# Turning the normalised x2 by two transposing DMAs instead of eight PE transposes and an ACT copy

## The reference

```python
x = x + 0.5 * ffn(layernorm(x))    # first expert layer
x = x + attn(layernorm(x))         # differential attention, 16 heads, 4 key/value heads, causal
x = x + 0.5 * ffn(layernorm(x))    # second expert layer, same weights

def ffn(x):                        # xf: 4096 tokens x 512
    logits = xf @ router_w + router_b          # 16 experts
    S = softmax(logits)
    G, idx = top_k(S.T, 256)                   # each expert takes its 256 best tokens
    out = xf[idx] @ expert_w + expert_b        # one weight matrix for all experts
    y = zeros.at[idx].add(G * out)
```

## Time and profile before

| | |
|---|---|
| time, median of 3 runs | 1959.65 us (1959.47 to 1966.55) |
| the profiled execution | 1976.26 us |
| its span, first to last instruction | 1974.5 us |
| granted TensorE clock over the span | 0.835 of full speed |
| instructions | 44298 |

### The profile page before, as it was taken

One profiled execution on the slowest core, in us unless ns is written; L12 is line 12 of the kernel. 1 busy time (PEld: TensorE's weight loads), 2 busy tenths in 40 slices (PEclk: granted clock), 3 DMA queues, 4 the chain that ended last, 5 costly groups with the idle time before them and its releaser, 6 DMA issues. The chain is left out here.

```text
span 1974.5 us, 44298 instructions
## 1 busy us (share of the span) xinstructions
PE 1514.6 (77%) x10639; PEld 1050.2 (53%) x10682; DVE 1446.2 (73%) x5493; ACT 1259.9 (64%) x3422; POOL 1098.9 (56%) x1507
## 2 busy tenths in 40 slices
PE   2897434478888988888988888988988988885520
PEld 2543212256666666666666666666666766663210
DVE  6568211588789899889888898988899767751168
ACT  2253112488778888888878888888788767762120
POOL 4321222366567777768776777777777555552200
PEclk9899666788889898989998998999899667666655
DMA  7013311111111111111111111211111100000077
GB/s 283 1 47 129 108 34 42 34 27 36 32 29 52 47 41 41 50 47 49 44 52 41 47 41 47 52 47 43 47 47 41 38 21 16 16 16 32 32 259 265
DMA packets 179670, 117.25 MB, mean 59 GB/s; under 512 B 139170, under 2 KB 139554, under 8 KB 179619
## 3 DMA queue, kind: packets, MB, share of 16 engines
q1 hardware_dynamic: 179618, 116.65, 20.0%
HBM read 51.57 MB, written 33.55 MB: 43 GB/s over the span
## 5 line engine op out<-in xcount | busy, mean ns | idle before, releaser
L1401 ACT ACTIVATE ex<-bank,nbias 128x512 f32<-128x512 f32 (+3 forms) x1024 | 528.8, 539 | 64.9 <-DVE bank L1120 62.5
L1120 DVE TENSOR_SCALAR_CACHE_REDUCE bank<-bank,nesc 128x512 f32<-128x512 f32 (+3 forms) x1024 | 503.3, 551 | 61.5 <-PE bank L1547 60.9
L1577 PEld LDWEIGHTS bank<-vs,pr 128*128 128x128 f32 x2560 | 339.7, 208 | 22.8 <-issue 12.8
L1577 PE MATMUL bank<-vs,pr 128*128 (+1 forms) x2560 | 344.1, 286 | 8.4 <-issue 4.1
L1559 PE MATMUL bank<-cst,df 128*128 128x128 f32 x1280 | 267.2, 312 | 85.5 <-ACT pr L1418 84.8
L1300 POOL TENSOR_SCALAR ex<-ex,gam 128x128 f32<-128x128 f32 (+3 forms) x512 | 318.8, 635 | 0.0
L1545 PE MATMUL bank<-ks,qs 96*128 (+2 forms) x1024 | 266.4, 337 | 48.9 <-ACT ex L1401 46.7
L1418 ACT ACTIVATE pr<-bank 128x128 f32<-128x128 f32 (+3 forms) x512 | 232.3, 454 | 95.7 <-PE bank L1559 94.7
L1146 DVE CUSTOM_DVE_ANT_0 df<-ex 128x128 f32<-128x128 f32 (+3 forms) x512 | 259.8, 522 | 8.4 <-issue 3.7
L1559 PEld LDWEIGHTS bank<-cst,df 128*128 128x128 f32 x1280 | 170.5, 168 | 112.2 <-ACT pr L1418 95.6
L1401 ACT ACTIVATION_READ_ACCUMULATOR ex<-bank,nbias 128x1 f32 x1024 | 223.5, 218 | 0.0
(11 more groups left out here) (272 smaller groups left out, 2960.2 us busy)
## 6 DMA issues: line engine op xcount, KB each, us to landing
qs<-turned SPq DMA_DIRECT2D x384, 64.0 KB, 2.1
x_dram<-xa SPq DMA_DIRECT2D x8, 1024.0 KB, 4.9
b_xs<-x_dram SPq DMA_DIRECT2D x32, 256.0 KB, 2.7
x<-x_dram SPq DMA_DIRECT2D x32, 256.0 KB, 2.6
x_dram<-x SPq DMA_DIRECT2D x32, 256.0 KB, 2.0
y_dram<-scratch SPq DMA_DIRECT2D x32, 256.0 KB, 2.0
c_x<-x_dram SPq DMA_DIRECT2D x8, 1024.0 KB, 14.5
c_y<-y_dram SPq DMA_DIRECT2D x8, 1024.0 KB, 15.2
```

The source lines that it names most:

```text
L1120: dve.tensor_scalar(part, part, nesc[:, 0:1], None, ALU.mult, ALU.min, accum_out=nbias[:, j, i, a:a + 1]).then_inc(bias_done.sem, 1)
L1401: ac.activation(ex[j % 4][:, a, lo:hi], energy(j, i)[:, a, :], ACT.Exp, bias=nbias[:, j, i, a:a + 1], scale=-1.0, accum_out=esum[:, j, i, ...
L1577: mm = pe.matmul(bank[:, 7, t * DV:(t + 1) * DV], pr[j % 2][:, lo + k * P:lo + (k + 1) * P], val, start=(k == 0), stop=(k == t))
```

## The change

The eight PE transposes of `turn_x2` and the ACT copy `take_x2` go. SP gets a function `turn_x2` between the reload of x2 and the store of y: it waits for `product_o` (which reads the buffer that is overwritten) and for `low2`, and issues two DMAs with `transpose=True`, one for each f16 half, from `split[:, a, HEADS]` to `xt2`, block by block. `route` on PE waits for both DMAs of its tile (32 increments of the new semaphore `xt2_in`). ACT's writes into `split[:, 0, HEADS]` for later tiles (`rope_high(0)`, `high_heads`), which waited for the PE turn of the tile before, wait for its DMAs.

```diff
@@ -989,7 +989,7 @@
                 "rstd2_done"), sig("xn2_done")
             hi2_done, lo2_done, xt2_done, xt2_out = sig("hi2_done"), sig("lo2_done"), sig("xt2_done"), sig("xt2_out")
             route_done, lg_out, y_done, y_out = sig("route_done"), sig("lg_out"), sig("y_done"), sig("y_out2")
-            x2_st, y2_st = sem2("x2_st"), sem2("y2_st")
+            x2_st, y2_st, xt2_in = sem2("x2_st"), sem2("y2_st"), sem2("xt2_in")
             x1_t = x1_d.rearrange("b (t p) e -> (b t) p e", p=P)
             x2_t = x2_d.rearrange("b (t p) e -> (b t) p e", p=P)
             y2_t = y2_d.rearrange("b (t p) e -> (b t) p e", p=P)
@@ -1064,6 +1064,12 @@
                     x2_done.wait(sp, u, apart_s)
                     sp.dma_start(flat(x2_t[ds(u, 1), :, :]), x2[:, :]).then_inc(x2_st, 16)
 
+                def turn_x2(u):
+                    o_done.wait(sp, u, apart_s)
+                    lo2_done.wait(sp, u, apart_s)
+                    for a in range(2):
+                        sp.dma_start(xt2[:, a, :].rearrange("p (k n) -> p k n", k=KT), split[:, a, HEADS].rearrange("p (k n) -> p k n", k=KT), transpose=True).then_inc(xt2_in, 16)
+
                 def store_y(u):
                     y_out.wait(sp, u, apart_s)
                     sp.dma_start(flat(y2_t[ds(u, 1), :, :]), yb[:, :]).then_inc(y2_st, 16)
@@ -1090,6 +1096,7 @@
                     store(K - BEHIND)
                     if again:
                         load_again(K - (BEHIND - 1))
+                    turn_x2(K - BEHIND)
                     store_y(K - BEHIND)
                     if u is not None:
                         stack(u, K)
@@ -1442,7 +1449,7 @@
                             xt_done.wait(ac, tau)
                         if n == 0 and pi is not None:
                             ant_done.wait(ac, pi)
-                            xt2_done.wait(ac, pi - 1)
+                            ac.wait_ge(xt2_in, pi * 32)
                         ac.copy(split[:, 0, n * 512:n * 512 + width], rot[:, 0:width]).then_inc(rhi_done.sem, 1)
                     return f
 
@@ -1473,11 +1480,6 @@
                     ant_done.wait(ac, u)
                     y_done.wait(ac, u - 1)
                     ac.copy(at[:, :, :], post_pair).then_inc(at_out.sem, 1)
-
-                def take_x2(u):
-                    xt2_done.wait(ac, u)
-                    o_done.wait(ac, u)
-                    ac.copy(xt2[:, :, :], post_pair).then_inc(xt2_out.sem, 1)
 
                 def take_chunks(n):
                     c0, c1 = CHUNKS[n]
@@ -1511,12 +1513,12 @@
                 run_bodies(ac, [[(7, probs(1)), (0, exps(1)), (0, exps(0))], [(6, probs(0))], [(5, shift)]],
                            {1: [prep(take_x)], 5: [high_heads], 7: [rope_high(0)], 8: [post(take_heads)],
                             10: [prep(take_chunks(0))], 12: [rope_high(1)], 13: [high2], 15: [prep(values)],
-                            16: [post(take_x2)], 17: [rope_high(2)], 20: [prep(take_chunks(1))],
+                            17: [rope_high(2)], 20: [prep(take_chunks(1))],
                             21: [take_y, prep(take_chunks(2))]},
                            {20: [high]},
                            [(take_x, 0), (tile(rope_high(0)), 0), (tile(rope_high(1)), 0), (values, 0), (tile(rope_high(2)), 0),
                             (take_chunks(0), 0), (take_chunks(1), 0), (high, 1), (take_chunks(2), 0)], spread,
-                           [(take_heads, 0), (last(high2), 0), (take_x2, 0), (last(high_heads), 1), (last(take_y), 0)])
+                           [(take_heads, 0), (last(high2), 0), (last(high_heads), 1), (last(take_y), 0)])
 
             @blk.tensor
             def _(pe):
@@ -1651,13 +1653,8 @@
                     at_out.wait(pe, u)
                     three(pe, post_bank, *parts(at, wo_h, wo_l, 0, E)).then_inc(o_done.sem, 1)
 
-                def turn_x2(u):
-                    x2_done.wait(pe, u)
-                    lo2_done.wait(pe, u)
-                    turn(post_pair, HEADS, xt2_done)
-
                 def route(u):
-                    xt2_out.wait(pe, u)
+                    pe.wait_ge(xt2_in, u * 32 + 32)
                     three(pe, post_bank[:, 0:NX], *parts(xt2, wr_h, wr_l, 0, NX)).then_inc(route_done.sem, 1)
 
                 def expert(u):
@@ -1669,11 +1666,11 @@
                                 []],
                            {1: [prep(turn_x)], 5: [prep(project(0))], 7: [post(turn_heads), prep(project(1))],
                             10: [post(product_o)], 12: [prep(turn_chunks(0))], 13: [prep(project(2))],
-                            17: [post(turn_x2)], 19: [prep(turn_chunks(1))], 20: [post(route)], 21: [post(expert)],
+                            19: [prep(turn_chunks(1))], 20: [post(route)], 21: [post(expert)],
                             22: [prep(turn_chunks(2))]}, {},
                            [(turn_x, 0), (project(0), 0), (project(1), 0), (project(2), 0), (turn_chunks(0), 0), (turn_chunks(1), 0),
                             (turn_chunks(2), 0)], spread,
-                           [(turn_heads, 0), (product_o, 0), (turn_x2, 0), (route, 0), (expert, 0)])
+                           [(turn_heads, 0), (product_o, 0), (route, 0), (expert, 0)])
```

## The result

The changed kernel takes 1983.96 us in the median (1977.06 to 1987.71, 4 runs) against 1959.56 us for the kernel before (1954.23 to 1966.55, 4 runs). The ratio is 1.0108, with a 95% interval of 1.0082 to 1.0134: slower by about 1%, clear of the noise. The forecast was 1963 us, no change that can be measured, with a range of 1942 to 2100.

The account below looks back on a forecast made before the run. No engine was full; PE and DVE, near 90% busy in full bodies, were taken to bound it by handing work over. Terms -13 - 5 + 8 + 14 = +4 us gave 1963 against the median of 1959.65; range 1942 to 2100.

Parts of the forecast that it names:

- side of "slower": Whole kernel: slower by more than about 0.5% (9.8 us), chance 0.45, mainly by PE stalling in front of route.
- the room: Time from the end of low2 to the start of route: 4.5 to 6.2 us expected in bodies, 2.3 in closing loop.
- The forecast case: Whole kernel: 1963 us, no measurable change, own range 1952 to 1976, chance 0.30.
- L: Latency from the end of low2 until both DMA halves have landed: 5.2 us, between 3.0 and 9.0.
- Route against L: Bodies: where L exceeds the room, PE stalls before route and the stall passes in full to DVE, +8 us.
- Closing loop: Four closing steps and the last body before them: nothing hides L, +14 us in all.
- Bodies without a next tile: Five later bodies bound by PE, partly at 1.2 GHz: removed transposes and copy save 1.0 us each, -5 us.
- Full bodies: 22 full bodies: removing the PE transposes and ACT copy saves 0.6 us each, -13 us.
- Rival 4: Full bodies: one more stretch at 1.2 GHz in each, about 1.1 us, +24 us on top, 1987 us; chance 0.08.

Follow-up runs that it names:

- e14: e6 with the low half turned a second time by DMA after the first pair landed, route waiting for it: 1999.5 us, ratio 1.0206 to the kernel before.
- e3: Changed kernel with both the eight PE transposes and ACT work of about the old copy's length kept in the bodies: 1962.3 us, ratio 0.9997 to the kernel before.
- e15: Kernel before with eight useless PE transposes of weights in front of the wait of turn_heads in each body: 1952.1 us, ratio 0.9971 to the kernel before.
- e4: Changed kernel without the two transposing DMAs, so x2 is not turned at all: 1967.7 us, ratio 1.0031 to the kernel before.
- e1: Changed kernel with the eight PE transposes of x2 kept in the bodies, their result unused: 1945.4 us, ratio 0.9916 to the kernel before.
- e6: Changed kernel with eight useless PE transposes of weights per body in front of the wait of turn_heads: 1947.4 us, ratio 0.9918 to the kernel before.
- e2: Changed kernel with useless ACT copies of about the old copy's length in the bodies, route waiting for them: 1966.0 us, ratio 1.0020 to the kernel before.
- e10: Changed kernel with the useless PE transposes of both e1 and e6: 1944.7 us, ratio 0.9913 to the kernel before.
- e12: e6 with eight more useless PE transposes of weights at slot 15, once x2_done has come: 1943.1 us, ratio 0.9918 to the kernel before.
- e7: Kernel before with its eight PE transposes of x2 done twice in the bodies: 1966.7 us, ratio 1.0022 to the kernel before.

## Why the prediction was right or wrong

The result lies in the range, on the side of "slower", which had a chance of 0.45. But the mechanism that the prediction had for slower, a landing later than the room, did not occur in the bodies, so that side held by luck. The forecast case itself, no change, was wrong. Point by point:

- *L.* Predicted 5.2 us, between 3.0 and 9.0. Measured 3.9. The two issues take 1.25 us each, where 0.72 per 64 KB was taken from the `qs` DMAs (2.9 for all, against 2.5). The sum also let the 2.1 us of landing begin when the last issue had ended; the row counts from the start of an issue, so the last issue was in it twice, and rightly added the same rows give 4.5. By the Trainium skill (VectorE: DVE Perf Modes, The three transpose paths) eight blocks in series would have given 12.8 us, an estimate from its 1309 ns a block; the trace shows both DMAs, eight blocks, landed after 3.9, so its price does not add up block by block. The other rule (Trainium skill, Advanced Engine Details and Errata, X-Bar Transpose), that they are as fast as regular DMAs, holds for the landing, 2.5 us against the 2.6 of the plain 256 KB loads of x between 700 and 1500 us, not for the issue, 1.25 us against 0.36.
- *Route against L, +8 us.* Nothing, since L is shorter than the room. The room was mis-sized too: 4.5 to 6.2 us predicted, 5.5 to 6.0 measured, so that even L = 5.2 would have fitted. e14 shows that the mechanism is right; what share of a stall passes on stays open.
- *Closing loop, +14 us.* The size followed L: 1.6 us a step instead of 2.9. In the profile three steps lost 6.5 us, 2.2 each, and what follows 1.6. In e3, with the same loop at another clock, the three lost 2.3.
- *Bodies without a next tile, -5 us.* -4.1 measured, in part by luck: the same five bodies took 217 us in the kernel before, and 204 in e15, which only adds work to it, as the clock was 0.70 or 0.78.
- *Full bodies, -13 us.* This is the step that failed: "I take 0.6, the PE time itself: 22 x 0.6". The upper bound came from a DVE wait of 1.0 us in a body that had two stretches at 1.2 GHz. At full clock there is no such wait to win: the body takes 42.1 us with and without the turn (e4), so the term is zero. The mean of 44 us that looked like slack on DVE was the price of the slow stretches. Measured, the 21 full bodies did not gain but lost 9.8 us in the profile, and the clock, which the sum put at nothing, is what made them lose it.
- *Rival 4, the clock.* That is what decided, with a chance of only 0.08. Its number, 1987, is close to the 1984 measured, but by luck: it contains -13 and +8 us that did not occur, and one more stretch in each body, where the profile has a quarter of one and other places. Its reason, less PE work and a wait in its place, holds in part. e1 and e6 put PE work back and lost slow stretches. But e2 adds no PE work and has just as much slow time, in cheaper places: when PE's work comes counts, and not only how much there is.

In e1 and e6 eight f16 transposes in a gap raised the median granted clock from 0.834 to 0.863 and 0.860, and the time fell from 1984 to 1945 and 1947 us. The Trainium skill (TensorE: Matmul & The Clock Gate, Part 4: PE-mode transpose) says that the full clock does not engage for transposes. By that a filler of transposes should give nothing back, and e1 and e6 would have stayed at 1984 us or above. The measurement decides for this kernel.

What stays open: why the filler of e6 helps the changed kernel and not the one before (e15), and why a second filler adds nothing to the time (e10, e12), can be told after the fact from where the stretches lie in each profile, but was not forecast from the work in the gaps. e2, faster with more ACT work, has no explanation beyond that place. And of the 24 us between the medians, the 14 beyond the profiles' 9.7 are in no row; only the listed clocks bear on them.

## What to carry to other kernels

When an engine's granted clock varies within the loop, price a saving from a body at full clock: cut the profile at the clock's changes, compare the floor of each version, and look at which matmuls run in the slow stretches. Work taken off PE can be worth nothing or less than nothing if another engine sets the floor and the slow stretches come to lie on dense work. Two short experiments settle it: put the removed work back as a filler, and remove it altogether; here the first was 16 us faster than the kernel before, and the second 6 us slower.

## What the runs showed of the hardware

- A transposing DMA of 128 x 512 f16 within SBUF occupied SP for 1.25 us (1.20 to 1.37, 64 of them) and landed 2.5 us after its issue in the median (2.4 to 4.1), the same in full bodies as in the closing loop.
- Two such DMAs per body, 256 KB, cost the other engines nothing that could be measured (e3, ratio 0.9997, 0.9980 to 1.0014).
- A stretch of 3.4 us at 1.2 GHz lengthened a full body of 42.1 us by about 1.0 us (4 us after `head_norm`), by about 1.7 (at 17) or by 0.1 to 0.9 (at 25 to 28), the same in all profiles that have such a body, but for e14 with its stall.
- Eight useless 128 x 128 f16 transposes, 0.6 us of PE in each body, made the changed kernel some 37 us faster (e1, e6) and brought the one before no gain that could be measured (e15; 0.2% slower in e7).
- The same closing loop took 72.4 us for three steps in the changed kernel and 68.2 in e1, at a granted clock of 0.62 and 0.68.
